# One-core AdaLN block (attention and eight routed experts): the first group's four heads stored and loaded ahead of the rest, stack rows with their terms as neighbours, and the experts' bias fold done in the last batch's body

## The reference

```python
scores = einsum('bhid,bhjd->bhij', Q, K) / scale
scores = scores + lam * einsum('bhie,bhje->bhij', tanh(Q) @ J, tanh(K))
probs  = softmax(where(causal, -inf, scores))
x = x + ga * (probs @ V @ Wo.T + bo)
h = layernorm(x) * (1 + cb) + sb
# expert e:  xs + relu(((xs - mu) * rsqrt(var + eps) * gamma[e] + beta[e]) @ W1[e].T + b1[e]) @ W2[e].T + b2[e]
y = expert output of the row's argmax;  x = x + gb * (alpha * y + (1 - alpha) * h)
```

## Time and profile before

| | us |
|---|---|
| median of 3 runs | 809.66 (809.44 to 812.22) |
| profiled execution, its own time | 811.99 |
| its span | 810.2 |
| PE busy | 693.0 (86%) |
| DVE busy | 545.7 (67%) |
| ACT busy | 503.0 (62%) |
| POOL busy | 259.3 (32%) |
| mean granted TensorE clock | 0.94 of full |

### The profile page before, as it was taken

One profiled execution on the slowest core, in us unless ns is written; L12 is line 12 of the kernel. 1 busy time (PEld: TensorE's weight loads), 2 busy tenths in 40 slices (PEclk: granted clock), 3 DMA queues, 4 the chain that ended last, 5 costly groups with the idle time before them and its releaser, 6 DMA issues.

```text
span 810.2 us, 17292 instructions
## 1 busy us (share of the span) xinstructions
PE 693.0 (86%) x5199; PEld 344.7 (43%) x5199; DVE 545.7 (67%) x1249; ACT 503.0 (62%) x1182; POOL 259.3 (32%) x342
## 2 busy tenths in 40 slices
PE   4467999999999999978999998799798889897594
PEld 2252434334334434423344343244343225886594
DVE  6959667787856777745568767478587611798352
ACT  1440677676688767745877676466576578657372
POOL 2028129000214724330156253200344100456543
PEclk9866799999999999978999999799899799999898
DMA  8995914193260708260516093526123353533510
GB/s 226 320 177 216 157 32 133 55 186 76 51 118 2 234 4 157 44 189 29 94 26 210 3 157 60 173 52 121 33 100 100 111 181 96 162 94 118 178 57 10
DMA packets 54723, 92.04 MB, mean 114 GB/s; under 512 B 10161, under 2 KB 26061, under 8 KB 54120
## 3 DMA queue, kind: packets, MB, share of 16 engines
q1 hardware_dynamic: 48444, 79.72, 39.4%
q0 software_dynamic: 3520, 8.42, 3.1%
q10 hardware_dynamic: 2668, 2.78, 1.2%
HBM read 51.04 MB, written 37.90 MB: 110 GB/s over the span
## 4 chain that ended last, share of the span: by engine, by line
PE 55%; DVE 18%; issue 10%; ACT 8%; DMA 4%; another core or an unknown queue 2%; POOL 1%; DVEq 1%; ACTq 1%; SPq 0%; POOLq 0%
PE PS L1248 14%; PE PS L1208 13%; PE PS L1274 13%; ACT arenaA L1030 5%; DVE PS L1694 4%; PE PS L1325 3%; PE PS L1336 3%; DVE block_max L1701 3%; PE PS L1278 2%; DVE arenaA L1371 2%; DVE arenaB L1371 2%; ACT arenaB L948 2%; PE PS L1213 2%; DMA arenaB<-r_den 1%
## 5 line engine op out<-in xcount | busy, mean ns | idle before, releaser
L1030 ACT ACTIVATE arenaA<-PS 128x512 f32<-128x512 f32 (+3 forms) x768 | 333.1, 495 | 188.3 <-PE PS L1278 127.3
L1694 DVE CUSTOM_DVE_ANT_0 PS<-PS,mask 128x1024 f32<-128x1024 f32 (+3 forms) x256 | 261.7, 1035 | 119.0 <-PE PS L1208 104.8
L1274 PE MATMUL PS<-arenaA 99*128 99x512 bf16 (+3 forms) x768 | 228.9, 342 | 30.7 <-ACT arenaA L1030 18.7
L1208 PE MATMUL PS<-arenaA 96*128 96x512 bf16 (+3 forms) x768 | 207.5, 347 | 30.3 <-DVE block_max L1701 10.0
L1274 PEld LDWEIGHTS PS<-arenaA 99*128 99x128 bf16 x768 | 73.2, 99 | 223.7 <-ACT arenaA L1030 143.7
L1248 PE MATMUL PS<-arenaA,Vs 128*9 128x512 f32 (+3 forms) x1536 | 161.1, 496 | 0.0
L1701 DVE TENSOR_REDUCE block_max<-PS 128x8 f32<-128x1024 f32 (+1 forms) x96 | 100.4, 1046 | 37.6 <-PE PS L1213 30.5
L1208 PEld LDWEIGHTS PS<-arenaA 96*128 96x128 bf16 x768 | 68.6, 102 | 99.9 <-DVE maxima L1694 30.5
L1278 PE MATMUL PS<-after,identb 128*128 128x128 bf16 x512 | 105.7, 224 | 0.0
L842 POOL DMA_INDIRECT out_dram<-arenaA x46 | 46.7, 1016 | 103.2 <-DVE arenaA L1371 94.8
L1079 ACT ACTIVATE arenaA<-PS,b1p 128x128 f32<-128x128 f32 x184 | 52.7, 373 | 34.5 <-PE PS L1325 20.1
(11 more groups left out here) (219 smaller groups left out, 687.8 us busy)
## 6 DMA issues: line engine op xcount, KB each, us to landing
arenaA<-k_parts SPq DMA_DIRECT2D x96, 128.0 KB, 8.2
arenaA<-by_expert SPq DMA_DIRECT2D x46, 192.5 KB, 3.7
o_raw<-OT SPq DMA_DIRECT2D x32, 256.0 KB, 3.3
k_parts<-arenaB SPq DMA_DIRECT2D x24, 256.0 KB, 3.8
arenaA<-q_parts SPq DMA_DIRECT2D x16, 384.0 KB, 4.9
q_parts<-arenaB SPq DMA_DIRECT2D x18, 256.0 KB, 3.7
arenaA<-in_L_ffn_W_dram SPq DMA_DIRECT2D x2, 2048.0 KB, 13.2
arenaA<-q_parts SPq DMA_DIRECT2D x16, 256.0 KB, 5.7
```

The lines of the kernel that those rows point to most:

```text
L1030: a.activation(PT[:, u % EB, h, off:HALF], PS[:, 4 + n % SB_, off:HALF], ACT.Exp).then_inc(exp_ok, 1)
L1208: last = mm(PS[:, place + c0 // HALF, at:at + c1 - c0], SQ(g, h)[0:KROWS, t * P:(t + 1) * P], SK(g, h)[0:KROWS, c0:c1], start=(at == 0), s ...
L1274: last = mm(bank[:, off:HALF], SK(g, h)[0:MROWS, kb * P:(kb + 1) * P], SQ(g, h)[0:MROWS, qc * HALF + off:(qc + 1) * HALF], start=True, sto ...
L1694: v.tensor_tensor_reduce(out=src, in0=src, in1=mask[:, S - n:S], scale=1.0, scalar=-3e38, op0=ALU.add, op1=ALU.max, accum_out=maxima[:, pl ...
```

## The change

1. **The first group first.** In batch 0 the parts of heads 0 to 3 are stored in twelve smaller transfers ahead of the rest (`store_first`, `first_k_out` on SP, `first_q_out` on ACT), and group 0 is loaded once these have landed. Of its q side SP issues terms 0, 2, 4 and ACT terms 1, 3, 5. The other 12 heads are stored afterwards, all by SP, and group 1 is loaded when they have landed.
2. **Row terms as neighbours.** In every batch a load is of one term (`load_term`), six for q and six for k, and row `r` of term `t` goes to partition `6 r + t`, where it was `16 t + r`. The same rows meet in the matmul, in another order.
3. **W2 later.** Its load is issued behind group 0's loads; its eight turns follow chunks 13 to 20.
4. **The fold later.** `fold_beta` no longer runs in the prologue. W1 is loaded again in the last batch, in two halves (`load_fold`), into a free part of `arenaB`, with the matching half of beta; b2 is loaded there too. POOL folds one half ahead of `send_rows(B - 2)` and one behind it. ACT waits for `b1_ok` after the last batch's attention, and the beta and b2 loads of the prologue are gone.
5. `send_maxima` of group 0 stands between the two stores of turned weights.

```diff
+        def load_term(queue, b, g, side, t):
+            queue.dma_start(stacks[t:KROWS:TERMS, g, side, :, :],
+                            (q_parts, k_parts)[side][bass.ds(b, 1), g * HG:(g + 1) * HG, PART_OF[side][t], :, :].rearrange("a h r q -> (a r) h q"))\
+                .then_inc(stack_in[g], 16)
...
+        FIRST_HEADS = ((0, HG), (HG, H))
+        def store_first(queue, n, heads, done):
+            k, dst, off = TENSORS[n]
+            h0, h1 = heads
+            for j in range(3):
+                queue.dma_start(dst[0, h0:h1, j, off:off + HD, :], T16[h0 * HD:h1 * HD, k, j, :]).then_inc(done, 16)
...
-            sp.dma_start(Aap[:, 20480:24576].rearrange("p (e f) -> p e f", e=E), W2.rearrange("e d n -> d e n")).then_inc(w2_in, 16)
-            Q_ROWS = ((0, 0, 3), (3, 0, 2), (5, 0, 1))
...
-                for j in range(3):
-                    sp.dma_start(dst[0, :, j, off:off + HD, :], T16[:, k, j, :]).then_inc(parts0_k, 16)
-            sp.wait_ge(parts0_k, PARTS_OUT // 2)
+                store_first(sp, n, FIRST_HEADS[0], first_k_out)
+            sp.wait_ge(first_k_out, PARTS_OUT // 2)
             load_side(0, 0, 1)
-            sp.wait_ge(parts0_q, PARTS_OUT // 2)
-            load_side(0, 0, 0)
+            sp.wait_ge(first_q_out, PARTS_OUT // 2)
+            for t in (0, 2, 4):
+                load_term(sp, 0, 0, 0, t)
+            sp.dma_start(Aap[:, 20480:24576].rearrange("p (e f) -> p e f", e=E), W2.rearrange("e d n -> d e n")).then_inc(w2_in, 16)
+            for n in (1, 2):
+                store_first(sp, n, FIRST_HEADS[1], parts0_k)
+            for n in (0, 3):
+                store_first(sp, n, FIRST_HEADS[1], parts0_q)
             sp.wait_ge(va_ok, 1)
             load_values(0)
+            sp.wait_ge(parts0_k, PARTS_OUT // 2)
+            sp.wait_ge(parts0_q, PARTS_OUT // 2)
             load_group(0, 1)
...
+            def load_fold(part):
+                experts = slice(part * E // 2, (part + 1) * E // 2)
+                if part:
+                    sp.wait_ge(b1_ok, part)
+                sp.dma_start(W1F.rearrange("p (e c) d -> p e (c d)", c=FC), W1[experts].rearrange("e (p c) d -> p e (c d)", c=FC)).then_inc(fold_in, 16)
+                sp.dma_start(BETA, beta[experts].rearrange("e d -> (e d)").rearrange("(a n) -> a n", a=1).to_broadcast([P, E // 2 * D])).then_inc(fold_in, 16)
...
+                    if body == "last" and g == 0:
+                        load_fold(0)
+                        sp.dma_start(b2_b[:, :], b2.rearrange("e d -> (e d)").rearrange("(a n) -> a n", a=1).to_broadcast([P, E * D])).then_inc(b2_in, 16)
+                    if body == "last" and g == 2:
+                        load_fold(1)
...
+            fold_beta(0)
             send_rows(B - 2)
+            fold_beta(1)
...
+            act.wait_ge(first_q_out, PARTS_OUT // 2)
+            for t in (1, 3, 5):
+                load_term(act, 0, 0, 0, t)
...
-            turned_weights = 0
+            turned_weights, W2_FROM = 0, 13
```

More of the change, by code:

```diff
@@ L136, in build @@
         PAYI = Bap[:, 5120:5120 + TB * ROWW].bitcast(I32).rearrange("p (t w) -> p t w", w=ROWW)
+        FOLD = 5120 + TB * ROWW
+        W1F = Bap[:, FOLD:FOLD + E // 2 * FF].rearrange("p (k d) -> p k d", d=D)
+        BETA = Bap[:, FOLD + E // 2 * FF:FOLD + E // 2 * (FF + D)]
+        assert FOLD + E // 2 * (FF + D) <= 11264
+        FOLD_LINKS = 9
         WOG = sb("WOG", [P, B, D])
@@ L401, in _ @@
             sp.dma_start(W1r.rearrange("p (e c) d -> p e (c d)", e=E), W1.rearrange("e (p c) d -> p e (c d)", c=FC)).then_inc(w1_in, 16)
-            sp.dma_start(Aap[:, 20480:24576].rearrange("p (e f) -> p e f", e=E), W2.rearrange("e d n -> d e n")).then_inc(w2_in, 16)
-            Q_ROWS = ((0, 0, 3), (3, 0, 2), (5, 0, 1))
-            K_ROWS = ((0, 0, 1), (1, 0, 1), (2, 0, 1), (3, 1, 1), (4, 1, 1), (5, 2, 1))
             def load_side(b, g, side):
[L407 to L411, removed]
+                for t in range(TERMS):
+                    load_term(sp, b, g, side, t)
             def load_group(b, g):
@@ L676, in _, with fold_beta @@
-            fold_beta()
+            def fold_beta(part):
+                pool.wait_ge(fold_in, (part + 1) * 2 * 16)
+                w1 = W1F.rearrange("p (e c) d -> p e c d", c=FC)
+                beta_b = BETA.rearrange("p (e o d) -> p e o d", e=E // 2, o=1).to_broadcast([P, E // 2, FC, D])
+                links = part * FOLD_LINKS
+                for k in range(2):
+                    g.tensor_tensor(w1[:, 2 * k:2 * k + 2], w1[:, 2 * k:2 * k + 2], beta_b[:, 2 * k:2 * k + 2], ALU.mult).then_inc(b1_step, 1)
+                links, width = links + 2, D // 2
+                while width:
+                    pool.wait_ge(b1_step, links)
+                    g.tensor_tensor(W1F[:, :, 0:width], W1F[:, :, 0:width], W1F[:, :, width:2 * width], ALU.add).then_inc(b1_step, 1)
+                    links, width = links + 1, width // 2
+                pool.wait_ge(b1_step, links)
+                mine = slice(part * E * FC // 2, (part + 1) * E * FC // 2)
+                g.tensor_tensor(b1p[:, mine], W1F[:, :, 0], b1c[:, :, :].rearrange("p e c -> p (e c)")[:, mine], ALU.add).then_inc(b1_ok, 1)
+                assert links == (part + 1) * FOLD_LINKS
@@ L1070, in _ @@
             attention(B - 1, "last")
+            act.wait_ge(b1_ok, 2)
             def hidden(n):
@@ L1200, in maximum @@
                 if k == 0:
-                    pe.wait_ge(stack_in[g], (loads + 1) * 9 * 16)
+                    pe.wait_ge(stack_in[g], (loads + 1) * 12 * 16)
                 n = (t + 1) * P
@@ L1232, in _ @@
                     modulations()
-                for _ in range(6 if i == len(PREP) - 1 else 1 if i >= len(PREP) and turned_weights < 16 else 0):
+                for _ in range(6 if i == len(PREP) - 1 else 1 if i >= len(PREP) + (0 if turned_weights < 8 else W2_FROM) and turned_weights < 16 else 0):
                     turn_weights(turned_weights)
```

43 lines of the change are left out of this document (12 added, 31 removed).

## The result

The changed kernel takes 819.27 us (median of 6, 816.27 to 823.37), the kernel before on the same chip 809.55 (6 runs, 807.47 to 812.22): ratio 1.0116, 95% interval 1.0082 to 1.0150. It is slower by 9.7 us. I had forecast 805.7 and a range up to 812.5, so the prediction was wrong in size and in sign.

The account below looks back on a forecast made before the run. The prediction took the prologue's transfers, unexplained waits in the loop and the last batch's reciprocals chain as the limits. -4.4 + 2.9 - 3.0 + 0.5 = -4.0 took the profiled 811.99 to 808.0, median 805.7; likeliest range 803 to 808.5, all 799.5 to 812.5.

Parts of the forecast that it names:

- The last batch: Fold and b2 loads ahead of the reciprocals on SP's queue delay these by about 0.5 us: plus 0.5 (bounds 0 and 5).
- rival D: Slower, 811 to 815 us: slow stack loads in the last batch make the reciprocals come 5 us later; chance 0.15.
- First heads first: Prologue: smaller first q stores land at 42.5 instead of 44.96 us, a gain of 2.5 (bounds 0 and 4).
- Terms as neighbours: Prologue: stack loads at 350 GB/s instead of 202; with the earlier stores, chunk 0 moves from 51.74 to 47.3, minus 4.4.
- W2's turns later: Prologue: half clock in early chunks (plus 1.5) and turns behind chunk 13 (plus 1.4): plus 2.9 us (bounds 0 and 6.2).
- The loop: Shorter load bursts cut three unexplained waits, 12.75 us together, by a quarter: minus 3.0 us (bounds 0 and 9).

Follow-up runs that it names:

- fold_early_again: The changed kernel without part 4 (fold, beta and b2 in the prologue again), run again in the later session: 808.92 us, 0.9998 of before.
- neighbours_again: The kernel before with part 2 alone (each stack load writes 16 partitions, 6 apart), run again: 810.26 us, 1.0010 of before.
- b2_late: The changed kernel without part 4, but b2's load issued where the change has it, ahead of the reciprocals' store: 810.96 us, 1.0000 of before.
- fold_by_pool: The changed kernel with GpSimd issuing all five fold and b2 transfers and doing both folds ahead of the last but one batch's rows: 812.82 us, 1.0041.
- fold_on_act: The changed kernel with the first half's two loads and b2 issued on ScalarE's queue at the start of the last body: 814.07 us, 1.0043.
- fold_past_recip: The changed kernel with the first half's two loads and b2 issued behind the reciprocals' store and load, all else as changed: 816.38 us, 1.0065.
- after_again: The changed kernel itself, unaltered, run again beside other variants: 819.02 us, 1.0098 of the kernel before.
- fold_late_alone: The kernel before with part 4 alone (loads, folds and b2 in the last body): 789.56 us, 1.0091 of before in its session.
- early_all_heads: The changed kernel without part 4 and with part 1 undone, each first store carrying all heads: 809.28 us, 0.9980 of before.
- early_w2_first: The changed kernel without part 4 and with part 3 undone, W2 loaded behind W1 and turned at the old places: 809.19 us, 0.9988.
- fold_early: The changed kernel without part 4 (fold, beta and b2 in the prologue again): 779.75 us, 0.9959 of before in its session.
- b2_behind: The changed kernel with b2's load alone moved behind the reciprocals' store and load: 818.48 us, 1.0092 of before.

## Why the prediction was wrong

The cut of the span for the runs of the session with 810 us, as in the first table:

| | first tile | loop | last batch | rest | span |
|---|---|---|---|---|---|
| before | 84.7 | 468.5 | 26.7 | 230.3 | 810.2 |
| `fold_early_again` | 82.5 | 466.9 | 26.5 | 229.3 | 805.2 |
| `neighbours_again` | 82.0 | 468.6 | 26.3 | 232.7 | 809.6 |
| `b2_late` | 81.6 | 468.9 | 29.3 | 230.2 | 810.0 |
| `fold_by_pool` | 81.6 | 469.1 | 28.9 | 230.3 | 809.8 |
| `fold_on_act` | 82.8 | 472.2 | 29.4 | 231.1 | 815.5 |
| `fold_past_recip` | 82.8 | 468.7 | 33.6 | 229.8 | 814.8 |
| after | 81.6 | 469.5 | 35.6 | 231.0 | 817.7 |

- **The last batch, +0.5: the step that failed.** Measured +8.9 (+9.3 in `after_again`). The mechanism is that of rival D, to which I gave 0.15, and its 5 us for this delay were too small: 6.4, and 2.5 more behind it. I priced the queue only up to the load of the reciprocals (555.87). What was held is the small store in front of it, issued at 553.62 before, and the load can't be issued until this has landed. Two numbers were wrong besides. I put the stack loads at 350 GB/s, done at 549.5 with room for the fold's data; in fact SyncE needs some 0.68 us for each (twelve are issued in 8.2 us, from 540.45 to 548.66). The values' load, the last of the group, was issued at 548.72, 1.9 us later than the 546.83 of the earlier trace rows, and only 2.4 us ahead of the half's store, where it had been 6.4. And I let 1.83 MB finish at 383 GB/s without counting what they share the engines with: POOL, which waits for W1 and beta, started at 557.91. Rival D was tied to slow group loads; here the group loads land fast and are slow to issue, and `fold_late_alone`, with the old loads, has a smaller delay (6.69 us).
- **The half clock behind that wait** was not in any term, and costs 1.3 us. From the multiply to POOL's moments it is 8.6 us at clock 1.00 in before, `fold_early_again`, `early_all_heads` and `early_w2_first` (the multiply waited 0.52 to 1.18 us), and 9.9 us at clock 0.83 in `b2_late`, `fold_by_pool` and `fold_on_act` (1.94 to 3.34 us), which have no fold on POOL at that time. DVE is busy 7.8 us in all of them. The windows over it, of `fold_early_again` and of `b2_late`, with the clock ahead of the last two columns:

```profile
557.40:566.10 8.70, 7.93 (x80) 4.90 (x78) 7.87 (x21) 4.01 (x12) 0.05 (x1) 1.00 0.02 5
```

```profile
560.00:570.00 10.00, 8.43 (x66) 5.11 (x66) 7.89 (x21) 2.70 (x9) 0.10 (x1) 0.83 0.02 4
```

- **First heads first, 2.5 of the 4.4 us: nothing.** The landing, 43.62, was 1.1 later than the 42.5 forecast. Whole stores with the new loads do as well: with all 16 heads in each store (`early_all_heads`) they landed at 42.98 (38.00 + 4.98), and chunk 0 came at 49.72, against 50.02 in `fold_early_again`; in the two runs of part 2 alone they landed at 43.44 and 43.60. The four heads' stores do hold the engines low. With the last k load issued before 39.4, in 42 to 43 us the share is 0.25, four of 16 engines, where it is 0.86 with whole stores; first the changed kernel, then `early_all_heads`:

```profile
42.00:43.00 1.00, 1.00 (x7) 1.00 (x6) 0.93 (x3) 0.00 (x0) 0.00 (x0) 0.50 0.25 98
```

```profile
42.00:43.00 1.00, 1.00 (x7) 1.00 (x6) 0.93 (x3) 0.00 (x0) 0.00 (x0) 0.50 0.86 318
```

  That agrees with the Trainium skill (DMA: Bandwidth & Descriptors, "Why a DMA increments its semaphore by 16 and not by 1"), and it eats what fewer bytes give.
- **Terms as neighbours, the other 1.9 us: right in size, by a wrong rate.** Alone it brings chunk 0 to 49.54 and 49.82, 2.2 and 1.9 us early, and the first tile to 81.78 and 82.01. All of the prologue's gain is this part's, and the other parts may take some of it back: in the ten traces with parts 1 to 3, the q loads land 3.9 to 6.1 us after their last issue (2.8 and 2.9 with part 2 alone), chunk 0 starts at 49.2 to 51.4 and attention at 81.6 to 84.0, half of them after 82.6. What differs there is that W2's 2 MB and the later stores are issued right behind these loads; that they are the cause is not shown. The median landing of a k load fell from 8.2 us to 2.7; the page's part on DMA issues, before and after:

```profile
arenaA<-k_parts SPq DMA_DIRECT2D x96, 128.0 KB, 8.2
```

```profile
arenaA<-k_parts SPq DMA_DIRECT2D x96, 128.0 KB, 2.7
```

  The engines do the same bytes in little more than half of their time: share 0.57 at 163 GB/s in 540 to 552, against 0.99 at 167 in 543 to 553.5 before. That bears out the Trainium skill (SBUF — State Buffer, "Door 1: The DMA port swizzle"). But 128 KB (131 kB) for each 0.68 us of issue are 193 GB/s, and rates of 163 to 182 came, not 350. With the engines busy only 0.57 to 0.60 of the time, this fits loads that wait for their issues.
- **W2's turns later, a loss of 2.9: nothing.** From chunk 0 to the first tile it is 32.4 us in the change (31.9 to 33.3 in the ten traces), 33.0 before, 33.1 with W2 as before (`early_w2_first`). The clock came as forecast: 0.50 in 58.0 to 66.2, where the kernel before had 1.00 (though not from 52 on: 0.53 in 49 to 55), and 0.88 in 66.3 to 79.8, where it had 0.50, since the turns now lie there. The low stretch has moved ahead, and what it cost there and gave back here is not to be told apart. Nothing is what my lower bound said.
- **The loop, 3.0 us: nothing.** Its gaps of PE stand at 2.46, 2.69, 2.92 and 5.57 us. By the chain the loop's waits of over 2 us add up to 14.3 (2.46, 2.69, 3.65, 5.53), against 15.6 before: the prediction counted 2.49, 4.38 and 5.88 and passed over one of 2.85 at 378.33, so that the earlier trace rows are not the longest three. A burst of group loads that runs alone has fallen in share from 1.07 to 0.60, but the one around the longest gap has not grown lighter, as the window of the changed kernel says against the earlier trace rows:

```profile
504.00:514.00 10.00, 1.66 (x8) 0.96 (x9) 2.18 (x4) 2.20 (x5) 4.45 (x5) 0.69 0.87 275
```

  What causes the gaps stays open; no edit took them away. In the session in which the kernel before was 27 us shorter, the loop of `fold_early` has one such wait, of 2.63 us. Of the 22 us by which its profile is shorter than that of `fold_early_again`, 15 are the loop and 9 the rest, less 2 of the prologue.

The sum for the profiled execution was 808.0, and its own time was 819.5. Of these 11.5 us, 8.4 are the last batch (8.9 for 0.5), 4.0 the loop (+1.0 for -3.0) and 0.6 the rest, less 1.6 of the prologue (3.1 for 1.5). That the prologue came near its forecast is luck: the stores' gain and the late turns' loss were both nothing and nearly cancel.

No kernel that ran in two sessions beats the one before in both: `fold_early`, the change without part 4, was at 0.9959 in one and 0.9998 in the other. The changed kernel was at 1.0098 and 1.0116.

## What to carry to other kernels

A transfer that nobody waits for still has a place in a queue and takes engine time: before a load is moved, list what is issued within its duration behind it, on every queue, and who waits for that. A small store whose landing gates the next issue is the most exposed; here 1792 KB ahead of 64 KB made it land in 9 to 10 us in place of 2 to 4. And a stretch in which an engine idles 48 us is not room by itself. In the change the fold's loads could only be issued at its end, and where GpSimd issued them in time (`fold_by_pool`), they held up other transfers. Of the places tried here, only in the prologue did the fold cost nothing that could be measured: with it taken out (`fold_late_alone`) the first tile stood at 84.75, against 84.69.

## What the runs showed of the hardware that I had not expected

- A stack load of 16 partitions that stand 6 apart takes longer to issue than one of 16 neighbours with the same bytes (median 594 against 426 ns). These are the rows of the line for all of one execution, after and then before (duration in ns: shortest/median/longest):

```profile
L395 SPq DMA_DIRECT2D arenaA<-k_parts x96: 3/594/855, 35.0 to 548.1; - x96
```

```profile
L409 SPq DMA_DIRECT2D arenaA<-k_parts x96: 5/426/2347, 35.5 to 546.5; - x96
```

- DVE's multiply of two operands in SBUF takes 1.22 to 1.23 us in all kernels in which POOL is idle at that time, and 1.63, 1.71, 2.25 and 3.02 us in after, `after_again`, `fold_late_alone` and `b2_behind`, where POOL's fold runs beside it. In `b2_behind`:

```profile
563.17 6.89 POOL L705 TENSOR_TENSOR arenaB<-arenaB 128x1024 f32<-128x1024 f32 x7
563.57 3.02 DVE L1406 TENSOR_TENSOR arenaB<-arenaB 128x1024 f32<-128x1024 f32 x1 [5.04 <-DMA arenaB<-r_den]
```

  The Trainium skill (SBUF — State Buffer, "Who interferes with whom") says that a VectorE instruction with two SBUF inputs contends with a GpSimd instruction that reads SBUF, because the second input comes through a read interface that they share. The trace agrees, on both sides: POOL's seven adds of the fold take 6.88 to 6.89 us beside the multiply, and 6.04 to 6.08 in the kernels in which they run at another time. So the fold had a price beside DVE too.
